# Values ahead of the projection chunk, and both exponentials ahead of its copy, in the slots of an attention stage

## What is computed

```python
q = shape(x @ Wq)          # 16 heads of 64
k = shape(x @ Wk)
v = shape(x @ Wv)
scores = jnp.einsum('bhqd,bhkd->bhqk', q, k)
weights = jax.nn.softmax(scores + position_bias, axis=-1)
context = jnp.einsum('bhqk,bhkd->bhqd', weights, v)
return context @ Wo        # added to x, with a gate
```

## Time and profile before

| | us |
|---|---|
| median of 3 runs | 1002.38 |
| lowest and highest | 1001.78, 1007.32 |
| the profiled execution, its own time | 1003.77 |
| its span, first to last instruction | 1002.0 |
| TensorE busy with matmuls | 907.5 |
| ScalarE busy | 645.6 |
| VectorE busy | 607.9 |
| GpSimd busy | 272.4 |

### The profile page before, as it was taken

The page is one execution under the profiler, slowest core; times in us unless marked ns, Lnnn a source line. Parts: engine busy times, 40 slices in busy tenths (PEclk is TensorE's granted clock), DMA queues, the critical chain, the costliest instruction groups (busy, mean ns, idle before and its releaser), DMA issues. The chain is left out here.

```text
span 1002.0 us, 25392 instructions
## 1 busy us (share of the span) xinstructions
PE 907.5 (91%) x10220; PEld 666.4 (67%) x10220; DVE 607.9 (61%) x1369; ACT 645.6 (64%) x1101; POOL 272.4 (27%) x328
## 2 busy tenths in 40 slices
PE   7888619836999999999999999999999999998987
PEld 5566517714677777776777777677776777776776
DVE  5266601157566666666666666666675666667975
ACT  2544204316787787778878778778878877885343
POOL 1100360050332413233142332423234142214110
PEclk8899859957999999999999999999999999999999
DMA  8300322110002000200200100020020002000000
GB/s 258 123 1 2 158 65 65 48 42 1 2 1 89 2 2 2 89 1 3 89 2 2 72 18 2 2 89 2 2 89 2 2 2 39 2 2 2 1 16 27
DMA packets 27128, 35.48 MB, mean 35 GB/s; under 512 B 6042, under 2 KB 21716, under 8 KB 26836
## 3 DMA queue, kind: packets, MB, share of 16 engines
q1 hardware_dynamic: 25988, 31.76, 9.5%
q0 software_dynamic: 1024, 2.10, 0.7%
HBM read 28.48 MB, written 5.37 MB: 34 GB/s over the span
## 5 line engine op out<-in xcount | busy, mean ns | idle before, releaser
L533 DVE CUSTOM_DVE_ANT_0 soft<-SC,strips 128x1024 f32<-128x1024 f32 x256 | 303.3, 1222 | 79.0 <-PE SC L375 78.9
L494 ACT ACTIVATE soft<-soft,nmax 128x1024 f32<-128x1024 f32 x256 | 294.0, 1149 | 3.6 <-DVE nmax L533 3.6
L411 PE MATMUL CX<-PTs,V 128*64 128x256 f32 x2048 | 244.7, 381 | 0.0
L479 ACT COPY PTs<-PT 128x1024 f32<-128x1024 f32 x128 | 129.6, 1013 | 138.5 <-PE PT L394 138.5
L375 PE MATMUL SC<-qk 64*128 64x512 f32 x1536 | 212.1, 408 | 7.3 <-DVE nmax L533 7.0
L394 PEld LDWEIGHTS PT<-ident,soft 64*128 64x128 f32 x4096 | 158.9, 139 | 70.0 <-issue 34.8
L411 PEld LDWEIGHTS CX<-PTs,V 128*64 128x64 f32 x2048 | 142.7, 137 | 92.7 <-issue 35.0
L541 DVE COPY PTs<-PT 128x512 f32<-128x512 f32 x128 | 88.5, 692 | 161.0 <-PE PT L394 161.0
L394 PE MATMUL PT<-ident,soft 64*128 64x64 f32 x4096 | 176.3, 226 | 3.7 <-ACT PTs L486 2.4
L375 PEld LDWEIGHTS SC<-qk 64*128 64x128 f32 x1536 | 137.2, 188 | 32.8 <-issue 5.2
L322 POOL CAST qk<-raw_qk 128x512 fp32r<-128x512 f32 x60 | 36.8, 613 | 260.2 <-ACT raw_qk L298 260.2
(11 more groups left out here) (242 smaller groups left out, 1008.9 us busy)
## 6 DMA issues: line engine op xcount, KB each, us to landing
strips<-bias_vec SPq DMA_DIRECT2D x8, 1920.0 KB, 6.9
arena<-in_L_ffn_w SPq DMA_DIRECT2D x1, 2048.0 KB, 10.0
slots_in<-arena SPq DMA_DIRECT2D x1, 1536.0 KB, 9.0
arena<-slots_in SPq DMA_DIRECT2D x8, 192.0 KB, 3.6
slots_out<-arena SPq DMA_DIRECT2D x8, 192.0 KB, 2.0
x<-in_L_attn_x SPq DMA_DIRECT2D x2, 512.0 KB, 4.9
out<-x SPq DMA_DIRECT2D x4, 256.0 KB, 2.3
arena<-in_L_wmod SPq DMA_DIRECT2D x2, 384.0 KB, 5.5
```

Of the source, the lines that this page charges most:

```text
L411: ins = pe.matmul(CX[hd * DK:(hd + 1) * DK, 0:2 * P], V1[:, vb, t, hd * DK:(hd + 1) * DK], PTs[:, g % 2, hd, t, :], start=(t == 0), stop=( ...
L479: act.copy(turned_out(n, 0), turned_in(0)).then_inc(ev("ptA_out"), 1)
L494: act.activation(soft[:, n % RING, hd, :], soft[:, n % RING, hd, :], ACT.Exp, bias=nmax[:, j:j + 1], scale=-1.0, accum_out=rsum[:, hd, n % ...
L533: dve.tensor_tensor_reduce(soft[:, n % RING, hd, :], SC[hd][:, :], strips[:, u // B % 2, hd, i * P:i * P + S], 1.0, 3.4e38, ALU.add, ALU.m ...
```

## The change

In `pe_slot` the values are issued ahead of the middle work, in place of behind it. In `act_slot` the second exponential of the slot is issued ahead of the copy that empties the middle work, in place of behind it. Nothing else differs.

```diff
@@ pe_slot
             if 0 <= n < TILES:
                 pe_turn(pe, n, 0)
+            if 2 <= n < TILES + 2:
+                pe_values(pe, (n - 2) // 2, n % 2)
             what, a, c = middle(n)
             if what == "chunk":
                 pe_chunk(pe, a, c)
             elif what == "turn":
                 pe_weights(pe, a)
-            if 2 <= n < TILES + 2:
-                pe_values(pe, (n - 2) // 2, n % 2)
             if 0 <= n < TILES:
                 pe_turn(pe, n, 1)
             if n >= 4 and n % 2 == 0:
@@ act_slot
             if n + 2 < TILES:
                 act_exp(act, n + 2, 0)
+                act_exp(act, n + 2, 1)
             what, a, c = middle(n)
             if what == "chunk":
                 act_chunk(act, a, c)
@@
                 act.copy(wT[:, 4 * a:4 * a + w, :].rearrange("p w d -> p (w d)"), MI[:, 0:w * P]).then_inc(ev("wT_ready"), 1)
-            if n + 2 < TILES:
-                act_exp(act, n + 2, 1)
             if 0 <= n < TILES:
                 act_turned_half(act, n)
```

## The result

The changed kernel takes 1029.3 us (median of 4 runs, 1024.52 to 1033.95) against 1002.08 before: ratio 1.0268, 95% interval 1.0201 to 1.0335. That is 27 us slower, with 20 to 34 inside the interval; the forecast was 1026.6, 24 us slower.

A forecast was written before the change was run, and what follows sets the result against it. TensorE, busy in all 627 us of the steady part, was taken to bound the kernel; 29 x 0.80 + 1.05 = 24.2 us of projection waits, other terms zero, raised the median from 1002.38 to 1026.6 us, range 1020 to 1033.

The forecast's parts named there:

- The projection's wait: Output projection in even slots waits for ScalarE's later chunk copy: 29 x 0.80 us plus 1.05 in slot 120, 24.2.
- The order of values and chunk: TensorE's values ahead of the chunk, in itself: taken at zero, at most 4.7 us either way over 94 slots.
- Odd slots: No projection ends these slots, so the late chunk copy meets no waiter: taken at zero.
- The end: In slot 125 values wait for VectorE's second output copy, the transpose comes behind: at most 0.3 us, left out.
- Repaid: Idle of weight loads before the values, 29.7 us, comes back against 24.2: 5.5 us faster, about 997; chance 3%.
- The wait never appears: The chunk copy gets in ahead of the output projection: about 1002 us; chance 2%.
- lateness spreads: Values of even slots also wait on ScalarE's context copy: 9 us more in 30 slots, about 1036; chance 8%.
- The clock falls: TensorE's scores run at the low clock behind each wait: about 44 us more, about 1070; chance 2%.

The follow-up runs named there:

- Odd slots only: Both edits applied in odd slots alone, even slots as in the kernel before: 1001.39 us, ratio 1.0009.
- the exponentials alone: Only ScalarE's half of the change (second exponential ahead of the chunk copy), TensorE's order as in the kernel before: 1025.28 us, ratio 1.0244.
- the copy last: The changed kernel with the chunk copy one place later still, behind the half copy: 1044.21 us, ratio 1.044.
- the old copy order in even slots: The changed kernel with the chunk copy back between the two exponentials in even slots, values ahead of the chunk everywhere: 1014.59 us, ratio 1.0119.

## Why the prediction was right, step by step

**The projection's wait.** Right in place, count and cause: 29 waits on the chunk copy and one on the weights' copy. Forecast was 0.79 us in slot 24. The copy came where it was reckoned (3.91 us behind the turn in both), and the handover took 0.14, not 0.17, so the projection was 0.76 late (1.31 - 0.55). The 0.11 to the weight load was right (383.19 to 383.30 in slot 24 of the changed kernel). The 0.06 from load to matmul came from a projection that had not waited; behind a wait it is 0.03, in that slot and already in the restart of the earlier trace rows, whose first matmul starts at 252.89. Behind it, projection to scores took 0.44 in place of 0.42. Slot 120 took 6.53 against 5.49 from first turn to first turn, 1.04 more, where 1.05 was forecast. Stage: 24.4, forecast 24.2. By the pitch of the wide copies, 22.7 of it lie in the 29 slots (0.78 each, where 0.80 was taken), 1.0 in slot 120, and 0.7 in all the other slots together, some 0.01 each, which the sum had at zero. So the agreement to 0.2 us has some luck in it: two small errors of opposite sign. Odd slots only and the exponentials alone show that the projection's wait is the cause of the whole.

**The order of values and chunk.** Taken at zero, and it is: values pitch 381.06 - 379.28 = 1.78 and chunk 0.96, 2.74 together, against 0.91 + 1.83 = 2.74. The 0.05 moved from one block to the next. I had asked the profile for a values pitch near 1.88 behind the turn. That was wrong: 1.88 was the price with a turn on both sides.

**Odd slots.** Taken at zero, and shown so by the run with odd slots only (655.09 against 655.08). The reason that I gave, that ScalarE does the same work ahead of the half copy, was only half of it. It holds since the second exponential covers the time until the moved chunk arrives. Without it the odd slots are the dearer place, 33 us.

**The end.** At most 0.3 us, left out. The values in slot 125 waited longer for VectorE, as said, but from slot 124's wide copy to slot 127's it is 16.5 us in both kernels: nothing. The timeline of the changed kernel there answers to the earlier trace rows:

```profile
938.03 1.95 PE L411 MATMUL CX<-PTs,V 128*64 128x256 f32 x16 [0.79 <-DVE wo_out L549]
939.91 0.33 PE L445 MATMUL MI<-ident,strips 128*128 128x128 f32 x1
```

**The rivals.** *Repaid* falls: the weight loads' idle time before the values did go (it is absent from the changed kernel's waits between 320 and 907 us, 29.7 us before), and the stage did not get shorter by it. In part it only moved: from 240 to 960 us the weight loads of the transposes idle 72.3 us in place of 54.7. With odd slots only, 16.7 us in 59 places are left before the values, of 33.1 in 116 in the same stretch (255 to 882 us), and the time is unchanged. The Trainium skill's rule in Perfetto Trace Analysis, section Identifying the Most-Contended Engine, that matmul busy time is a poor measure of the limit, did not bring slack here: with weight loading at 72% before, the projection's lateness was still paid in full. *The wait never appears* and *lateness spreads* fall by the waits view: the values wait once, in slot 125, and the first turns wait for the half copy twice, 2.2 us in all, as they did before (twice, 2.4). *The clock falls* falls too: 1.00 over the steady part with the idles of 0.6 us in it, and 1.00 with those of 1.3 us in the run with the copy last.

**The 6 us outside the stage.** In the profiled execution of the changed kernel slot 1 began 4.4 us later (its wide copy started at 252.93 against 248.51), of which slot 0 to slot 1 took 1.6, and behind slot 127 lie 1.4 more. Windows view of the changed kernel at the stage's start:

```profile
245.00:250.00 5.00, 3.77 (x41) 3.37 (x38) 3.46 (x7) 3.75 (x7) 0.00 (x0) 0.50 0.00 0
```

TensorE was at the 1.2 GHz level there, where before it was granted 1.00 from 244 us on in slots 0 and 1. Slot 0's second turn shows it, in the changed kernel and then in the kernel before:

```profile
247.41 1.12 PE L394 MATMUL PT<-ident,soft 64*128 64x64 f32 x16 [1.23 <-ACT PTs L479]
244.58 0.72 PE L394 MATMUL PT<-ident,soft 64*128 64x64 f32 x16 [1.22 <-ACT PTs L479]
```

The edited order has no part in this. Slots -2 to 0 have no chunk, and values begin in slot 2, so up to slot 1's wide copy all engines have the same lists in both kernels; behind slot 127 too. Slot 0 to slot 1 took 5.04 to 5.08 us in the kernel before and in five of the runs, the copy last among them, which has both edits. It took 6.68 in the changed kernel and 6.84 in the run with the old copy order in even slots, whose granted clock from 240 to 244 us was 0.50. So 1.6 us of the 6 are the clock at the start. The other 2.8 ahead of slot 0, and the 1.4 behind slot 127, were not traced further. The runs of the changed kernel spread from 1024.52 us, at a mean granted clock of 0.963, to 1033.95 at 0.952, and the profiled one is the slowest. Four such runs do not tell 24 from 27 us.

No version beats the kernel before. Its TensorE row is full in the steady part, so an order of the same instructions has no wait to remove there. What a block costs did move a little with its neighbours (values 1.78, 1.83 or 1.88 us), but in the run with odd slots only that came to nothing.

## What to carry to other kernels

When an engine is full, an edit of order has little to win and waits to lose, and what it loses can be reckoned before building it: list who waits on each moved instruction in the same slot, and compare the time at which it will be out with the time at which the full engine comes to the wait. Move things together with the filler that they need. Here one edit alone costs 45 us, the other 24, and both together 24: in even slots the shorter wait (0.3 us) disappears behind the longer (0.8), and in odd slots 33 us of waits are filled. If a copy must move behind longer work, move it only in the slots in which nobody needs it at once.

## What was not expected of the hardware

An exponential of 512 columns without a sum holds ScalarE for 0.62 us from start to start, emptying the 512 columns of a chunk for 0.48 (383.09 - 382.61 in slot 24 of the changed kernel), an exponential of 1024 columns with its sum for 1.14. And a TensorE block that waited is a little dearer at its end: projection to next scores takes 0.44 us against 0.42, and the first turn of the odd slot behind it 0.62 on average with the exponentials alone moved, against 0.59 before.
